# Two heads' states on the two halves of the partitions, instead of on a block diagonal

## The reference

```
xn = layernorm(x)
h  = rmsnorm(xn);  q, k, v = h @ ternary(qkv_w).T          # 16 heads of 64
for each chunk of 128 tokens, each sequence, each head:
    scores = (q k^T) * mask                                # decay inside the chunk
    o      = scale * (scores v + (q * lam_t) S)            # within the chunk + from the state
    S      = lam_T * S + (k * lam_rev)^T v                 # one decay, one addition
s = rmsnorm(rmsnorm(o)) @ ternary(proj_w).T
g = silu(xn @ ternary(ffn_w).T + bias)
out = x + s * g
```

## Time and profile before

| what | value |
|---|---|
| time, median of 3 runs | 1341.33 us (1341.18 to 1342.14) |
| the profiled execution: its time, its span | 1341.38 us, 1340.1 us |
| TensorE matmul, busy | 1312.0 us, 98% of the span |
| DVE, ACT, POOL, busy | 934.7, 583.5, 635.5 us |
| granted TensorE clock | full in all 40 slices |

### The profile page before, as it was taken

How to read it: one execution, slowest core, us unless ns; L and a number is a source line. 1 busy time by engine, 2 the same in 40 slices (tenths; PEclk the granted TensorE clock), 3 DMA queues, 4 the chain that set the end, 5 groups by cost and what they waited for, 6 DMA issues and landing times.

```text
span 1340.1 us, 25937 instructions
## 1 busy us (share of the span) xinstructions
PE 1312.0 (98%) x10409; PEld 842.5 (63%) x10409; DVE 934.7 (70%) x1489; ACT 583.5 (44%) x1139; POOL 635.5 (47%) x532
## 2 busy tenths in 40 slices
PE   4999999999999999999999999999999999999998
PEld 2577767674656657566675656657566575656655
DVE  7887467785666957667575776957667686776835
ACT  5884143343434544444353434544344453434521
POOL 1432877952544535447341654535435352654432
PEclk9999999999999999999999999999999999999999
DMA  9521111203021030300303021030301303020000
GB/s 363 234 95 64 72 33 38 97 17 119 2 71 64 17 118 1 121 15 17 118 17 118 2 96 40 17 119 1 127 9 21 114 17 119 1 88 17 33 32 32
DMA packets 33432, 90.32 MB, mean 67 GB/s; under 512 B 10529, under 2 KB 10785, under 8 KB 33314
## 3 DMA queue, kind: packets, MB, share of 16 engines
q1 hardware_dynamic: 33024, 88.65, 18.7%
q10 hardware_dynamic: 290, 0.02, 0.0%
HBM read 71.85 MB, written 16.81 MB: 66 GB/s over the span
## 4 chain that ended last, share of the span: by engine, by line
PE 89%; POOL 3%; DVE 3%; ACT 2%; issue 2%; DMA 1%; SPq 0%; POOLq 0%; ACTq 0%; DVEq 0%
PE ring L747 19%; PE ring L880 15%; PE ring L706 13%; PE ring L732 12%; PE ring L680 11%; PE att_ps L784 4%; PE att_ps L830 3%; PE att_ps L834 3%; PE ring L796 2%; PE att_ps L811 2%; PE ring L759 1%; POOL sq L2186 1%; PE ring L655 1%; DMA raw<-in_ffn_w 1%; ACT junk L1700 1%
## 5 line engine op out<-in xcount | busy, mean ns | idle before, releaser
L747 PE MATMUL ring<-b_lo,qkv_q 128*128 128x256 f16 x1216 | 268.2, 273 | 0.0
L747 PE MATMUL ring<-b_hi,qkv_q 128*128 128x256 f16 x1216 | 268.2, 272 | 0.0
L880 PE MATMUL ring<-proj_q,o_hi 128*128 128x512 fp8e4 x496 | 188.1, 379 | 3.0 <-DVE o_lo L1422 3.0
L880 PE MATMUL ring<-proj_q,o_lo 128*128 128x512 fp8e4 x496 | 188.0, 379 | 0.0
L2142 POOL TENSOR_TENSOR gate_even<-gate_even,bias 128x512 f32<-128x512 f32 x14 | 19.8, 1414 | 275.4 <-ACT gate_even L1819 275.4
L2182 POOL TENSOR_TENSOR sq<-sq,cols 128x1024 f32<-128x1024 f32 x29 | 55.1, 1900 | 165.5 <-DVE b_lo L1254 157.3
L747 PEld LDWEIGHTS ring<-b_hi,qkv_q 128*128 128x128 fp8e4 x1216 | 120.3, 99 | 15.6
L747 PEld LDWEIGHTS ring<-b_lo,qkv_q 128*128 128x128 fp8e4 x1216 | 118.9, 98 | 15.7
L2208 POOL TENSOR_TENSOR xt<-xt,gate_even 128x512 f32<-128x512 f32 x58 | 88.2, 1531 | 69.7 <-DVE gate_even L1442 68.5
L2186 POOL TENSOR_TENSOR sq<-sq 128x1024 f32<-128x1024 f32 (+1 forms) x58 | 109.5, 1888 | 4.5
L1843 ACT ACTIVATE gate_even<-gate_even 128x512 f32<-128x512 f32 x60 | 37.6, 629 | 154.7 <-DVE gate_even L1285 154.7
(11 more groups left out here) (257 smaller groups left out, 3249.1 us busy)
## 6 DMA issues: line engine op xcount, KB each, us to landing
xt<-in_x SPq DMA_DIRECT2D x62, 512.0 KB, 8.3
out<-xt SPq DMA_DIRECT2D x31, 512.0 KB, 3.1
raw<-in_qkv_w SPq DMA_DIRECT2D x24, 512.0 KB, 15.7
y<-in_x_turned SPq DMA_DIRECT2D x14, 512.0 KB, 6.8
y_odd<-in_x_turned SPq DMA_DIRECT2D x14, 512.0 KB, 7.7
raw<-in_ffn_w SPq DMA_DIRECT2D x8, 512.0 KB, 9.9
norm_rows<-norm_out SPq DMA_DIRECT2D x14, 256.0 KB, 6.0
raw<-in_proj_w SPq DMA_DIRECT2D x6, 512.0 KB, 4.5
```

Of the source, the lines that this page charges most:

```text
L747: ins = pe.matmul(ring[:, b, e * BT:(e + 1) * BT], qkv_q[:, cb, o:o + P], part[:, cb, :], start=(cb == 0 and part is b_hi), stop=(cb == NC ...
L880: ins = pe.matmul(ring[:, b, :], part[:, cb, :], proj_q[:, cb, cs], start=(cb == 0 and k == 0), stop=(cb == NCB - 1 and k == 1))
```

## The change

`state` is laid out as 8 tiles of 128x64: head 0's state on partitions 0 to 63, head 1's on 64 to 127, with no zeros between, and the memset and its semaphore go. The two products from the state read 64 rows each, of the state and of `q_decay`. The addition and the decay become one instruction of 128 partitions each, and the counts of `s_st` and `s_sd` are halved with them. In the sequence's very first chunk the copy waits for the last rounded weight tile instead of the memset.

```diff
-        state = arena[:, ST_OFF:SM_OFF].rearrange("p (k r e) -> p k r e", k=2, r=PR)
+        state = arena[:, ST_OFF:ST_OFF + 2 * PR * D].rearrange("p (k r e) -> p k r e", k=2, r=PR)
...
                     if not is_first(g):
                         for e in range(2):
-                            pe.matmul(att_ps[e * D:(e + 1) * D, half, j, :],
-                                      state[:, passes_on(g) % 2, r, e * D:(e + 1) * D], q_decay[:, r, :],
+                            rows = slice(e * D, (e + 1) * D)
+                            pe.matmul(att_ps[rows, half, j, :], state[rows, passes_on(g) % 2, r, :], q_decay[rows, r, :],
                                       start=True, stop=False, skip_group_check=True)
...
-                for e in range(2):
-                    rows, cs = slice(e * D, (e + 1) * D), slice(e * D, (e + 1) * D)
-                    to = state[rows, (n + 1) % 2, :, cs]
-                    if is_first(g):
-                        dve.tensor_copy(to, kv_ps[rows, :, :]).then_inc(s_st, 1)
-                    else:
-                        dve.tensor_tensor(to, to, kv_ps[rows, :, :], ALU.add).then_inc(s_st, 1)
+                to = state[:, (n + 1) % 2, :, :]
+                if is_first(g):
+                    dve.tensor_copy(to, kv_ps[:, :, :]).then_inc(s_st, 1)
+                else:
+                    dve.tensor_tensor(to, to, kv_ps[:, :, :], ALU.add).then_inc(s_st, 1)
...
-                for e in range(2):
-                    rows, cs = slice(e * D, (e + 1) * D), slice(e * D, (e + 1) * D)
-                    pool.tensor_tensor(state[rows, (n + 1) % 2, :, cs], state[rows, n % 2, :, cs],
-                                       lam_T[rows, :].unsqueeze(2).to_broadcast([D, PR, D]), ALU.mult).then_inc(s_sd, 1)
-
-                    pool.wait_ge(s_sd, 2 * (n - g // NCHUNK - 1) + e + 1)
+                pool.tensor_tensor(state[:, (n + 1) % 2, :, :], state[:, n % 2, :, :],
+                                   lam_T[:, :].unsqueeze(2).to_broadcast([P, PR, D]), ALU.mult).then_inc(s_sd, 1)
...
-            pool.memset(state, 0.0).then_inc(s_state0, 1)
```

More of the change, by code:

```diff
@@ L182, in program @@
         s_ident, s_iota, s_cut = sem("ident_made"), sem("iotas_made"), sem("mask_cut")
-        s_state0 = sem("state_zeroed")
         s_ones, s_peak = sem("constants_set"), sem("peak_taken")
@@ L776, in scores @@
                     if g > 0 and half == 1:
-                        pe.wait_ge(s_st, 2 * passes_on(g))
+                        pe.wait_ge(s_st, passes_on(g))
                         if c == 0 and aside(i - 1, 1):
@@ L805, in update_state @@
                 if n > 0:
-                    pe.wait_ge(s_st, 2 * n)
+                    pe.wait_ge(s_st, n)
                 for r in range(PR):
@@ L1381, in add_state @@
                 dve.wait_ge(s_kv, n + 1)
-                if n == 0:
-                    dve.wait_ge(s_state0, 1)
                 if is_first(g):
@@ L1386, in add_state @@
                         dve.wait_ge(s_o, HALF * g)
-                else:
-                    dve.wait_ge(s_sd, 2 * (passes_on(g) - (g // NCHUNK + 1)) + 2)
-                for e in range(2):
-                    rows, cs = slice(e * D, (e + 1) * D), slice(e * D, (e + 1) * D)
-                    to = state[rows, (n + 1) % 2, :, cs]
-                    if is_first(g):
-                        dve.tensor_copy(to, kv_ps[rows, :, :]).then_inc(s_st, 1)
-                    else:
-                        dve.tensor_tensor(to, to, kv_ps[rows, :, :], ALU.add).then_inc(s_st, 1)
+                    else:
+                        dve.wait_ge(s_wout, w_n["qkv", QKV_TILES - 1])
+                else:
+                    dve.wait_ge(s_sd, passes_on(g) - (g // NCHUNK + 1) + 1)
+                to = state[:, (n + 1) % 2, :, :]
+                if is_first(g):
+                    dve.tensor_copy(to, kv_ps[:, :, :]).then_inc(s_st, 1)
+                else:
+                    dve.tensor_tensor(to, to, kv_ps[:, :, :], ALU.add).then_inc(s_st, 1)
             def weight_o(i, c, half):
@@ L2164, in decay_state @@
                     pool.wait_ge(s_beta, chunk(i + 1, c) + 1)
-                pool.wait_ge(s_st, 2 * n)
+                pool.wait_ge(s_st, n)
                 pool.wait_ge(s_o, HALF * g)
-                for e in range(2):
-                    rows, cs = slice(e * D, (e + 1) * D), slice(e * D, (e + 1) * D)
-                    pool.tensor_tensor(state[rows, (n + 1) % 2, :, cs], state[rows, n % 2, :, cs],
-                                       lam_T[rows, :].unsqueeze(2).to_broadcast([D, PR, D]), ALU.mult).then_inc(s_sd, 1)
-                    pool.wait_ge(s_sd, 2 * (n - g // NCHUNK - 1) + e + 1)
+                pool.tensor_tensor(state[:, (n + 1) % 2, :, :], state[:, n % 2, :, :],
+                                   lam_T[:, :].unsqueeze(2).to_broadcast([P, PR, D]), ALU.mult).then_inc(s_sd, 1)
             def sum_squares(i, c):
```

## The result

The changed kernel takes 1399.73 us (median of 4 runs, 1399.20 to 1400.11) against 1341.26 us: a ratio of 1.0434, 95% interval 1.0421 to 1.0447. The forecast was 1401.3 us, in a range of 1377 to 1425. The profiled execution took 1399.20 us with a span of 1398.0, 57.9 more than before.

A forecast was written before the change was run, and what follows sets the result against it. TensorE was taken to bound the kernel, its matmuls busy 1312.0 of 1340.1 us. 1341.4 + 62.9 for changes of form - 3.0 for covered waits = 1401.3 us, range 1377 to 1425.

The forecast's parts named there:

- The count and the price of a change of form: TensorE's outputs: 419 more changes between 64*64 and 128*64 at 0.15 us each, 62.9 us.
- The entry into L830: Nearest measured change of form, into the outputs: gap 0.10 plus first weight load 0.05, 0.15 us.
- Neither bound: Limits for the 419 changes: low 39.0 us (gap alone, 0.093 each), high 83.8 us (0.20 each).
- the high bound: Each change priced as the entry into the scores, 0.09 gap plus 0.11 load: 83.8 us.
- the working on the scores: TensorE's detour through scores: 2.08 us for 16 steps of 0.11, taken as 0.30 over, in gaps and a load.
- The products themselves cost the same: State products of 64 rows in the outputs: no gain, still 0.218 us a block.
- What the longer outputs cover: TensorE ahead of L880: longer outputs cover five waits for `o_lo`, 3.0 us back; the `sq_sum` wait stays.
- One addition, one decay, no memset: State work on DVE and POOL: saves 19 and 27 us there, counted as nothing in the sum.
- the first estimate: POOL's saving from 24 fewer decays of 1.07 us and 1.8 us of memset: 27 us.
- The first rival: Outputs: changing rows alone is free at 64 columns; about 1341 us, or 1336; chance 0.10.
- The second rival: State blocks: two heads queue for one PSUM bank, 0.21 us more per block, 47 us, 1448 us; chance 0.09.

The follow-up runs named there:

- whole-chunk order: Changed kernel with all eight pairs' products from the state first, then all from the scores: 1344.72 us, ratio 1.0024 to the kernel before.
- four corners: Whole-chunk order with the second half's heads exchanged in PSUM and state products alternating between halves: 1328.00 us, ratio 0.9898 to the kernel before.
- two corners: Four-corner kernel without the exchange of heads, keeping the turns between two PSUM banks: 1345.01 us, ratio 1.0025 to the kernel before.

## Why the prediction was right

**The count and the price of a change of form** were both right: 419 changes at 0.15 us, 62.9 us forecast, against 2.24 us for 15 of them, which is 62.5 us over the 28 chunks (27 with 15, one with 14). The entry into L830, from 128*128 to 128*64, was the right row to price it by, and its two parts are found again: the last block has no change behind it and is still 0.26 long instead of 0.218, so about 0.05 is the load of first weights, and the other 0.10 is the gap. Neither bound was met: the first weights of a block are not loaded within the gap, and 64 columns of them cost 0.05 us and not the 0.11 that the high bound took from the scores. In the working on the scores, 2.08 us is 0.32 over 16 steps of 0.11, not 0.30; no term of the sum goes by it.

**The products themselves cost the same**, as assumed: 1.90 us for the state's 32 records in the whole-chunk order, of which 8 x 0.218 = 1.74 are the products, and 0.15 the load of the first weights and the gap ahead of the scores.

**What the longer outputs cover** was given as 3.0 us. All five waits for `o_lo` are gone and the wait for `sq_sum` stays, both as forecast. The span says that more came back: 62.5 - 57.9 = 4.6. First, the waits were worth more than the row of waits says, since it counts from the modelled end of the record before. From the last block of a sequence's outputs to L880 it was 357.76 - 356.86 = 0.90 us before and is 0.38 now, of which 0.05 is the load of weights:

```profile
369.99 0.44 PE L834 MATMUL att_ps<-arena 128*64 128x128 f32 x4
370.37 0.39 PE L880 MATMUL ring<-proj_q,o_hi 128*128 128x512 fp8e4 x1
```

That is 0.57 us, four times, and in block 1 it is 1.0: 3.3 us. Second, 0.8 us is the program's start, where the first product from the state begins at 114.4 instead of 115.2 us; in the run with the 64 rows alone it began at 116.3, so this differs from run to run by more than it explains. Third, one L868 at 212.8 us waits some 0.4 us less for POOL's `diag` (the two rows on `diag` above; the kernel before has the same 1.2 us there as the run with two additions). These make 4.5 of the 4.6. The prediction had the cover right and the other two at nothing.

**One addition, one decay, no memset** at nothing: right to within about a microsecond. The runs with the 64 rows alone and with the two additions and decays differ from the changed kernel by 0.6 and 1.1 us, with times that overlap. (With a slower decay POOL would have saved 21 us and not the 19 that the prediction gives, which left the memset out; it saved 27, as the first estimate said.)

**The first rival**, that rows alone change for free while the columns stay 64, is refuted by the blocks of 0.368 us. The Trainium skill, "TensorEngine Tiling (Array Packing)", section "Key Properties", says that a change of tiling mode drains TensorE. The trace now agrees for these two forms too, with 0.149 us for each change, of which 0.05 is a load of weights.

**The second rival**, that the heads queue for one bank, is refuted as well: 32 records of 128 columns in 1.90 us are two at once, since one by one, at 0.11 us, they would take 3.5. The Trainium skill, the same page, section "Gotcha 1: PSUM Pressure", says that different row tiles can't access one bank at the same time. Here the two heads of a pair do so, on different partitions of it and without loss, and the measurement decides.

## What to carry to other kernels

Count the changes of a product's form, rows by columns, along TensorE's order before making products smaller: here each cost 0.149 us, two thirds of the 0.218 us of a block of work, and TensorE's busy share of 98% hid it. If small products are wanted, put those of one form together and let them take all four corners; in this kernel leaving out the zeros gained nothing in itself (1344.7 us in the whole-chunk order), and the four products at once that it makes possible gained 17 us. And when a stretch of TensorE gets longer or shorter, look at what runs beside it: TensorE's waits for `o_lo` were 3.0 us before, none in the changed kernel and 9.8 us with four corners.

## What the hardware showed beyond that

Four 64*64 products on four corners run at once: 1.03 us for 32 records against 1.89 us on two corners. Gaps at every 0.37 us through stretches of 5.8 us didn't lower the granted clock: the window from 100 to 1380 us of the changed kernel has it at 1.00, the upper level of 2.4 GHz (behind the engines' busy times, ahead of the DMA share):

```profile
100.00:1380.00 1280.00, 1276.89 (x9804) 771.33 (x9803) 813.12 (x1306) 504.18 (x1044) 570.10 (x468) 1.00 0.15 52
```
